# A transformer-block kernel on one core: the first version's row of attention maxima issued by ScalarE, the projection weights on the same queue

## The chip, the cores and the metric

One core of one Trainium2 chip runs the whole program. The metric is device time in microseconds of that core. The kernel before takes 3811.2 us, the median of three runs (3807.66, 3811.2, 3812.2).

## The reference

The input is `x`, four images of 32 x 32 positions with 192 channels, so 4096 tokens. The block computes, one after the other:

```python
x = x + L0_conv(ln(x))      # attention over 1024 positions, 12 heads of 16, with
                            # relative position terms for row and column in the scores
t = t + L0_ffn(ln(t))       # 8 experts, the best 2 of them weighted
x = x + L1_conv(ln(x))      # as L0_conv
t = t + L1_ffn(ln(t))       # attention without position terms, MLP, 4 experts
```

The attention is

```python
attn = einsum('bnqd,bnkd->bnqk', q, k) * scale + bias     # bias: rel_h + rel_w, or none
attn = softmax(attn, axis=-1)
out  = einsum('bnqk,bnkd->bnqd', attn, v)
```

with 48 heads (4 images by 12) of 1024 queries by 1024 keys in each of the three attentions.

## The kernel before

The program is a row of stages with a barrier between them. Three of these are `attention` (line 509): `c0att` and `c1att` with position terms (`rel`), and `f1att` without. A stage works through 24 pairs of heads, and buffers turn in a ring of three (`RING`), so that pair p uses slot p % 3.

**Two streams run side by side in a stage.** The first finds, for every query, a maximum of approximate scores: TensorE multiplies queries by keys (`use_bank`, line 672) into one of three PSUM banks, and VectorE takes the maximum of each 128 x 512 tile (`dve_max`, line 734), 32 tiles for a pair. After the last tile VectorE joins the maxima (lines 739 and 743), TensorE turns them into rows (line 665), and ScalarE copies these out of PSUM into `mrow` (`act_row`, line 747). A DMA then puts the rows, as one row of `qa` on partition 96, beside the queries. With that row in the product the scores come out with the maximum already taken off. The second stream uses them, one pair later: TensorE computes scores of two heads (`score`, line 687), ScalarE their exponential (line 973), and TensorE multiplies by the values (`weigh`, line 700). A pair takes eight steps, `kt` = 0 to 7, one for 128 keys each.

**Versions.** With position terms the keys are split in four quarters, and `qa` holds four versions of the queries, each with its own position rows. Each version needs its own copy of the row of maxima. `place_rows` (line 617) issues them on SyncE's queue, version by version, two heads each: eight DMAs for a pair in `c0att` and `c1att`, two in `f1att`. Version 0 counts on the semaphore `s_at[0]`, the others on `s_at[1]`.

**What waits for what.** `score` at kt 0 waits for `s_at[0]` (line 679), and at kt 2, where version 1 begins, for `s_at[1]` (line 684). Ahead of kt 0, TensorE waits for `s_ld`, the landing of the pair's queries and keys (line 722). The scores of kt 0 belong to the pair before in TensorE's order: they are issued in its step 8. A score product of head h at kt waits for the exponential of the same head at kt - 1 (line 681), since it overwrites it in PSUM. A pair of maxima products waits until VectorE has released the banks (line 660). TensorE's order in one step is: scores of both heads, two maxima products, the weighing product, two maxima products.

**ScalarE's order** (`act_pair`, line 986): the two exponentials of each kt; after kt 0 the copy of the sums of the pair before, after kt 1 a DMA that stores them (line 983); after kt 5 (`ROWS`) the row of maxima of the next pair. At the stage's head it waits for the projection weights (`s_pw`), splits them (line 999), and copies the row of pair 0.

**SyncE's queue** (line 845): at the head the projection weights and the bias (three DMAs), then for each of the three slots the maxima's inputs (`load_maxima`) and the pair's inputs (`load`, 17 DMAs with position terms, nine without), then `refill` for each pair: `place_rows` of pair p - 1, which waits for ScalarE's copy, `load_maxima` of pair p + 1 (ten DMAs), `load` of pair p. GpSimd has a queue of its own, on which every three pairs the sums and their inverses come back.

At the head of a stage VectorE sets ones and zeros (lines 932 to 936), splits the weights (line 941), and then takes all 32 tiles of pair 0 and 14 of pair 1 before the first score product is in TensorE's order (`START`, line 635).

Of the kernel before, what the change touches and what calls it, by code (L numbers as in the profile page):

```python
# [22 lines left out]
B, SIDE, C, NH, HD = 4, 32, 192, 12, 16  # L23
L = SIDE * SIDE
T = B * L
P = 128
# [6 lines left out]
KT = L // P  # L33
QSIDE = SIDE // 2
# [3 lines left out]
HALF, HALVES = C // 2, 2 * B  # L38
# [5 lines left out]
R_REL = 0  # L44
R_QK = 64
R_MAX = 96
R_LOW = 97
# [461 lines left out]
def attention(nc, name, vt, rel, scratch, hot, ident16, by_pool, res, wo, bo, stats=None, room=None, spots=None, spare=None,  # L509
# [6 lines left out]
    with Pool(nc, name) as m:  # L516
        versions = QUARTERS if rel else 1
        qa = room or [m.sb(f"qa{u}", 2 * L, F16) for u in range(RING)]
# [10 lines left out]
        mrow = [m.sb(f"mrow{u}", P, F16, parts=2 * KT) for u in range(RING)]  # L529
# [4 lines left out]
        pw = m.sb("pw", 2 * C, parts=HALF)  # L534
        pwh, pwl = (m.sb(n, 2 * C, F16, parts=HALF) for n in ("pwh", "pwl"))
        bias = m.sb("bias", C)
# [6 lines left out]
        s_pw, s_pwh, s_pwl, s_bias = m.sem("pw"), m.sem("pwh"), m.sem("pwl"), m.sem("bias")  # L543
# [7 lines left out]
        s_ld = [m.sem(f"ld{u}") for u in range(RING)]  # L551
# [3 lines left out]
        s_m16, s_row, s_qm = m.sem("m16"), m.sem("maxrow"), m.sem("qamax")  # L555
        s_s, s_e, s_pv = m.sem("scores"), m.sem("exp"), m.sem("pv")
        s_o, s_at = m.sem("out"), [m.sem(f"maxplaced{k}") for k in range(2)]
# [7 lines left out]
        def queries(h, version, first, count):  # L565
            at = (h * versions + version) * L + first
            return slice(at, at + count)

        def load(sp, pair, u):
            heads = bass.ds(pair * 2, 2)  # L570
            for part, row in ((0, R_QK), (1, R_QK + HD), (0, R_LOW)):
                sp.dma_start(ka[u][row:row + HD, :].rearrange("p (h n) -> p h n", h=2),
                             scratch["qk"][1, heads, part, :, :].rearrange("h r n -> r h n")).then_inc(s_ld[u], 16)
            if not rel:
                for part, row in ((0, R_QK), (0, R_QK + HD), (1, R_LOW)):
                    sp.dma_start(qa[u][row:row + HD, :].rearrange("p (h n) -> p h n", h=2),
                                 scratch["qk"][0, heads, part, :, :].rearrange("h r n -> r h n")
                                 ).then_inc(s_ld[u], 16)
                return
            for h in range(2):  # L580
                head = bass.ds(pair * 2 + h, 1)
                to = qa[u][:, h * versions * L:(h + 1) * versions * L]
                for part, row in ((0, R_QK), (0, R_QK + HD), (1, R_LOW)):
                    src = scratch["qk"][0, head, part, :, :].rearrange("a r n -> (a r) n").unsqueeze(1)
                    sp.dma_start(to[row:row + HD, :].rearrange("p (v n) -> p v n", v=versions),
                                 src.broadcast_to([HD, versions, L])).then_inc(s_ld[u], 16)

                for k in range(2):
                    for half in range(2):
                        row = R_REL + 2 * QSIDE * k  # L590
                        src = scratch["rel"][head, k, half].rearrange("a p r n -> (a p r) n").unsqueeze(1)
                        dst = to[row:row + 2 * QSIDE, :].rearrange("p (u s n) -> p u s n", u=2, s=2)
                        dst = dst[:, half, :, :] if k == 0 else dst[:, :, half, :]
                        sp.dma_start(dst, src.broadcast_to([2 * QSIDE, 2, L])).then_inc(s_ld[u], 16)

        def load_maxima(sp, pair, u):

# [19 lines left out]
        def place_rows(sp, pair, u):  # L617

            sp.wait_ge(s_qm, pair + 1)
            for v in range(versions):  # L620
                for h in range(2):
                    sp.dma_start(qa[u][R_MAX:R_MAX + 1, queries(h, v, 0, L)],
                                 mrow[u][h * KT:(h + 1) * KT, :]).then_inc(s_at[v > 0], 16)

        EARLY = 14
        ROWS = 5
# [102 lines left out]
        def bank_of(u, item):  # L729
            return mps[(len(START) + len(USES) * u + USES.index(item)) % 3]  # L730
# [14 lines left out]
        def act_row(act, pair, u, bank):  # L745
            act.wait_ge(s_row, pair + 1)
            act.activation(mrow[u][:, :], bank[0:2 * KT, 0:P], ACT.Copy).then_inc(s_qm, 1)

        def dve_pair(dve, pair, u, skip=()):
            for item in USES:  # L750
                if item[0] not in skip and item[1] != "row":
                    dve_max(dve, pair + item[0], item[1], bank_of(u, item))
# [91 lines left out]
        with nc.Block() as block:  # L844
            @block.sync
            def _(sp):
                for j in range(2):
                    sp.dma_start(pw[:, j * C:(j + 1) * C], wo[j * HALF:(j + 1) * HALF, :]).then_inc(s_pw, 16)
                sp.dma_start(bias[:, :], bo.broadcast_to([P, C])).then_inc(s_pw, 16)
                for u in range(RING):  # L850
                    for h in range(2 if rel else 0):
                        sp.dma_start(km[u][64 * h + HD:64 * h + 64, :], spots).then_inc(s_lm[u], 16)
# [115 lines left out]
            def _(act):  # L968
# [17 lines left out]
                def act_pair(turn, pair, u, first=False, last=False):  # L986

                    for kt in range(KT):
# [6 lines left out]
                        if kt == ROWS and not last:  # L995
                            act_row(act, pair + 1, (u + 1) % RING, bank_of(u, (1, "row")))

                act.wait_ge(s_pw, 3 * 16)
                act.activation(pwh[:, :], pw[:, :], ACT.Identity, scale=W_SCALE).then_inc(s_pwh, 1)
                act_row(act, 0, 0, mps[START.index((0, "row")) % 3])  # L1000
# [712 lines left out]
```

## Time and profile before

| | |
|---|---|
| median of three runs | 3811.2 us (3807.66 to 3812.2) |
| the profiled execution, its own time | 3804.64 us |
| its span | 3803.1 us |
| TensorE matmul busy | 3146.3 us (83%) |
| VectorE busy | 2664.5 us (70%) |
| ScalarE busy | 2032.5 us (53%) |
| maxima of one attention stage on VectorE (line 734) | 768 tiles of 685 ns |
| exponentials of one attention stage on ScalarE (line 973) | 384 of 1021 ns |

The span goes from the first instruction to the last. An engine's share of it is a mean over stages of different kinds. The three attention stages take the greater part of the time, and the change touches only them.

### The profile page before, as it was taken

What the parts mean: (1) busy time and instruction counts of PE and PEld (TensorE: products, weight loads), DVE (VectorE), ACT (ScalarE), POOL (GpSimd) and SP (SyncE); (2) the same over time, 40 slices, a digit from 0 to 9 for tenths busy, and PEclk for the clock granted to TensorE, in tenths of its full rate; (3) what the DMA queues carried; (4) which work ended last, traced back from release to release, by engine and by line L of the source; (5) the groups of instructions that cost most, each with busy time, mean ns of one, the idle gap of its engine ahead of it and who ended that gap; (6) DMA issues with size and microseconds to landing.
All of it is one profiled execution on the core that took longest, in us unless ns stands there. A gap on an engine that the chain in (4) does not pass through costs nothing. (4 is left out here: it accounts for less than half of the span.)

```text
span 3803.1 us, 66407 instructions
## 1 busy us (share of the span) xinstructions
PE 3146.3 (83%) x20240; PEld 1407.1 (37%) x20240; DVE 2664.5 (70%) x5142; ACT 2032.5 (53%) x2719; POOL 278.2 (7%) x363
## 2 busy tenths in 40 slices
PE   4748999986999999464899998346999996869998
PEld 2422222233666666341222223221222224636666
DVE  5458899966666666445889896638999974556555
ACT  3516677764433333341667676343777773455554
POOL 0010111110000000001011111001111110000000
PEclk9759999997999999675999999576999998979999
DMA  2274667742000000037476764010111111020000
GB/s 59 99 173 83 139 133 144 142 92 72 21 0 0 0 0 0 25 102 173 82 139 131 140 141 98 8 67 27 48 51 44 53 40 28 1 63 9 4 8 13
DMA packets 179968, 251.98 MB, mean 66 GB/s; under 512 B 50974, under 2 KB 73646, under 8 KB 179850
## 3 DMA queue, kind: packets, MB, share of 16 engines
q1 hardware_dynamic: 155642, 213.65, 25.4%
q0 software_dynamic: 13104, 17.60, 2.3%
q10 hardware_dynamic: 11104, 19.28, 1.4%
q8 instruction: 59, 0.97, 0.1%
q14 instruction: 59, 0.48, 0.0%
HBM read 182.80 MB, written 66.65 MB: 66 GB/s over the span
## 5 line engine op out<-in xcount | busy, mean ns | idle before, releaser
L734 DVE TENSOR_REDUCE c1att_mx<-c1att_m 128x1 f32<-128x512 f32 x768 | 493.9, 685 | 64.9 <-PE c1att_m L672 59.7
L734 DVE TENSOR_REDUCE c0att_mx<-c0att_m 128x1 f32<-128x512 f32 x768 | 493.4, 685 | 61.9 <-PE c0att_m L672 56.8
L734 DVE TENSOR_REDUCE f1att_mx<-f1att_m 128x1 f32<-128x512 f32 x768 | 493.3, 685 | 26.5 <-PE f1att_m L672 21.8
L973 ACT ACTIVATE c1att_p<-c1att_s 128x1024 f32<-128x1024 f32 x384 | 372.1, 1021 | 155.7 <-PE c1att_s L687 155.6
L973 ACT ACTIVATE c0att_p<-c0att_s 128x1024 f32<-128x1024 f32 x384 | 372.1, 1021 | 151.9 <-PE c0att_s L687 151.7
L973 ACT ACTIVATE f1att_p<-f1att_s 128x1024 f32<-128x1024 f32 x384 | 372.1, 1021 | 119.6 <-PE f1att_s L687 118.6
L1392 ACT ACTIVATE f_s<-f_u 128x512 f32<-128x512 f32 x192 | 114.6, 597 | 373.5 <-PE f_u L1317 373.5
L1481 DVE SCALAR_TENSOR_TENSOR f_h<-f_u,f_s 128x512 f32<-128x512 f32 x192 | 132.6, 691 | 149.5 <-ACT f_s L1392 145.6
L1400 ACT ACTIVATE moe_h<-moe_u,moe_bu 128x512 f32<-128x512 f32 x192 | 136.5, 711 | 175.8 <-PE moe_u L1317 93.8
L700 PE MATMUL c1att_o<-c1att_p,c1att_vs 128*32 128x512 f32 x1536 | 208.5, 615 | 0.6 <-ACT c1att_p L973 0.6
L700 PE MATMUL c0att_o<-c0att_p,c0att_vs 128*32 128x512 f32 x1536 | 207.5, 613 | 0.6 <-ACT c0att_p L973 0.6
L700 PE MATMUL f1att_o<-f1att_p,f1att_vs 128*32 128x512 f32 x1536 | 206.3, 609 | 0.6 <-ACT f1att_p L973 0.6
L1330 PE MATMUL f_y<-f_dh,xt 128*128 128x192 f16 x1536 | 202.2, 247 | 2.2 <-DVE xt L1437 2.2
L687 PE MATMUL f1att_s<-f1att_qa,f1att_ka 113*128 113x512 f16 x768 | 203.1, 386 | 0.6 <-ACT f1att_p L973 0.3
L1330 PE MATMUL moe_y<-moe_dh,xt 128*128 128x192 f16 x1536 | 195.1, 246 | 0.0
L672 PE MATMUL f1att_m<-f1att_km,f1att_qm 16*128 16x512 f16 x768 | 154.8, 399 | 48.4 <-DVE f1att_ka L936 29.4
L672 PE MATMUL c0att_m<-c0att_km,c0att_qm 64*128 64x512 f16 x768 | 156.2, 403 | 43.4 <-DMA c0att_qm<-rel_parts 24.2
L672 PE MATMUL c1att_m<-c1att_km,c1att_qm 64*128 64x512 f16 x768 | 156.2, 403 | 43.1 <-DMA c1att_qm<-rel_parts 23.9
L1437 DVE TENSOR_TENSOR xt<-moe_h,xt 128x512 f16<-128x512 f32 x192 | 131.3, 691 | 86.3 <-ACT xt L1402 85.3
L1330 PE MATMUL f_y<-f_dl,xt 128*128 128x192 f16 x768 | 189.8, 247 | 0.0
L1330 PE MATMUL moe_y<-moe_dl,xt 128*128 128x192 f16 x768 | 188.9, 246 | 0.0
L687 PE MATMUL c0att_s<-xt,c0att_ka 113*128 113x512 f16 x512 | 135.9, 388 | 31.0 <-DMA xt<-c0att_mrow 28.7
(488 smaller groups left out, 5963.4 us busy)
## 6 DMA issues: line engine op xcount, KB each, us to landing
xt<-rel_parts SPq DMA_DIRECT2D x256, 128.0 KB, 7.4
xt<-qk_parts SPq DMA_DIRECT2D x192, 128.0 KB, 5.0
y<-rel_parts SPq DMA_DIRECT2D x128, 128.0 KB, 5.4
y<-qk_parts SPq DMA_DIRECT2D x96, 128.0 KB, 4.8
c0att_qm<-rel_parts SPq DMA_DIRECT2D x144, 64.0 KB, 2.2
c1att_qm<-rel_parts SPq DMA_DIRECT2D x144, 64.0 KB, 2.2
rel_parts<-c0qkv_rhi SPq DMA_DIRECT2D x48, 128.0 KB, 2.3
rel_parts<-c0qkv_rlo SPq DMA_DIRECT2D x48, 128.0 KB, 2.3
```

The source lines that it names most:

```text
L672: ins = pe.matmul(bank[:, :], qm[v][rows, q0:q0 + P], km[v][rows, c * CHUNK:(c + 1) * CHUNK], start=True, stop=True)
L687: ins = pe.matmul(sps[h][:, c * CHUNK:(c + 1) * CHUNK], ka[u][0:R_END, kcol], qa[u][0:R_END, queries(h, version, c * CHUNK, CHUNK)], start ...
L700: ins = pe.matmul(ops[row:row + 32, :], vs[u][:, (h * KT + kt) * 32:(h * KT + kt + 1) * 32], pr[h][kt % 2][:, c * CHUNK:(c + 1) * CHUNK], ...
L734: dve.tensor_reduce(mx[:, n:n + 1], bank[:, :], AX.X, ALU.max).then_inc(s_mx, 1)
L973: act.activation(pr[h][kt % 2][:, :], sps[h][:, :], ACT.Exp).then_inc(s_e, 1)
L1330: ins = pe.matmul(yps[q % 2][t // 2][:, (t % 2) * C:(t % 2 + 1) * C], hidden[q % 2][:, x], down[:, w], start=k == 0 and i == 0, stop=k == ...
L1392: act.activation(s_buf[i % 2][:, :], ups[i % ring][0][:, :], ACT.Silu, scale=1.0 / W_SCALE).then_inc(s_s, 1)
L1400: act.activation(h32[:, i % 2 * CHUNK:(i % 2 + 1) * CHUNK], bank[:, :], ACT.Gelu, bias=bias, scale=1.0 / W_SCALE).then_inc(s_h32, 1)
L1437: dve.tensor_tensor(hl[q % 2][:, cols], h32[:, i * CHUNK:(i + 1) * CHUNK], hh[q % 2][:, cols], ALU.subtract).then_inc(s_hl, 1)
L1481: dve.scalar_tensor_tensor(out=h32[:, i % 2 * CHUNK:(i % 2 + 1) * CHUNK], in0=ups[i % ring][1][:, :], scalar=1.0 / W_SCALE, in1=s_buf[i % ...
```

## The change

The two DMAs of version 0 move from SyncE's queue to ScalarE's, straight behind the copy that makes the row; SyncE keeps the other versions (six DMAs with position terms, none without). In between ScalarE waits for its own copy. The three DMAs of the projection weights and bias move from SyncE's queue to ScalarE's at the head of a stage. In `load` the same DMAs are issued in another order: by kind and then head, where it was head and then kind.

```diff
-            for h in range(2):
-                head = bass.ds(pair * 2 + h, 1)
-                to = qa[u][:, h * versions * L:(h + 1) * versions * L]
-                for part, row in ((0, R_QK), (0, R_QK + HD), (1, R_LOW)):
...
+            to = qa[u].rearrange("p (h v n) -> p h v n", h=2, v=versions)
+            for part, row in ((0, R_QK), (0, R_QK + HD), (1, R_LOW)):
+                for h in range(2):
...
         def place_rows(sp, pair, u):
 
             sp.wait_ge(s_qm, pair + 1)
-            for v in range(versions):
+            for v in range(1, versions):
                 for h in range(2):
-                    sp.dma_start(qa[u][R_MAX:R_MAX + 1, queries(h, v, 0, L)],
-                                 mrow[u][h * KT:(h + 1) * KT, :]).then_inc(s_at[v > 0], 16)
+                    place_row(sp, u, h, v)
+
+        def place_row(queue, u, h, v):
+            queue.dma_start(qa[u][R_MAX:R_MAX + 1, queries(h, v, 0, L)],
+                            mrow[u][h * KT:(h + 1) * KT, :]).then_inc(s_at[v > 0], 16)
...
             act.activation(mrow[u][:, :], bank[0:2 * KT, 0:P], ACT.Copy).then_inc(s_qm, 1)
+            act.wait_ge(s_qm, pair + 1)
+            for h in range(2):
+                place_row(act, u, h, 0)
...
             def _(sp):
-                for j in range(2):
-                    sp.dma_start(pw[:, j * C:(j + 1) * C], wo[j * HALF:(j + 1) * HALF, :]).then_inc(s_pw, 16)
-                sp.dma_start(bias[:, :], bo.broadcast_to([P, C])).then_inc(s_pw, 16)
...
+                for j in range(2):
+                    act.dma_start(pw[:, j * C:(j + 1) * C], wo[j * HALF:(j + 1) * HALF, :]).then_inc(s_pw, 16)
+                act.dma_start(bias[:, :], bo.broadcast_to([P, C])).then_inc(s_pw, 16)
                 act.wait_ge(s_pw, 3 * 16)
```

## Rows read from the trace of the kernel before

**Rows 1.** Groups by line: VectorE's maxima in steady stretches, `f1att` then `c0att` (busy, idle before).

```profile
L734 DVE TENSOR_REDUCE f1att_mx<-f1att_m 128x1 f32<-128x512 f32 x702 | 450.8, 684 | 16.8 <-PE f1att_m L672 12.2
...
L734 DVE TENSOR_REDUCE c0att_mx<-c0att_m 128x1 f32<-128x512 f32 x703 | 451.6, 685 | 37.8 <-PE c0att_m L672 32.9
```

**Rows 2.** ScalarE's copy of the rows by line: count, ns, first and last start.

```profile
L747 ACT ACTIVATE f1att_mrow<-f1att_m x23: 266/266/267, 2634.5 to 3117.8; 16x128 f16<-16x128 f32 x23
...
L747 ACT ACTIVATE c0att_mrow<-c0att_m x22: 266/266/267, 332.9 to 811.9; 16x128 f16<-16x128 f32 x22
```

**Rows 3.** TensorE's waits, steady stretches of `c0att` and `c1att` (total us, times, longest).

```profile
PE c0att_s L687 <- DMA xt<-c0att_mrow: 13.5, 6, 2.7
...
PE c0att_s L687 <- DMA xt<-rel_parts: 1.9, 1, 1.9
PE c0att_s L687 <- DMA y<-c0att_mrow: 1.9, 2, 1.1
...
PE c1att_s L687 <- DMA xt<-c1att_mrow: 10.5, 6, 2.3
PE c1att_s L687 <- DMA y<-c1att_mrow: 4.3, 2, 2.3
PE c1att_s L687 <- DMA y<-rel_parts: 2.0, 1, 2.0
```

**Rows 4.** The wait of SyncE's queue in steady `c0att` (total us, times, longest).

```profile
SPq L622 <- ACT c0att_mrow L747: 117.4, 23, 18.6
```

**Rows 5.** Timeline of one pair of `c0att` (start us, us, instructions, idle before).

```profile
514.09 0.27 ACT L747 ACTIVATE c0att_mrow<-c0att_m 16x128 f16<-16x128 f32 x1 [0.77 <-PE c0att_m L665]
...
514.38 5.42 SPq L622 DMA_DIRECT2D xt<-c0att_mrow  x8
...
514.70 1.94 ACT L973 ACTIVATE c0att_p<-c0att_s 128x1024 f32<-128x1024 f32 x2 [0.35 <-PE c0att_s L687]
...
515.47 5.21 DVE L734 TENSOR_REDUCE c0att_mx<-c0att_m 128x1 f32<-128x512 f32 x8 [0.48 <-PE c0att_m L672]
...
516.69 1.04 PE L687 MATMUL c0att_s<-xt,c0att_ka 113*128 113x512 f16 x4
...
517.66 0.39 PE L672 MATMUL c0att_m<-c0att_km,c0att_qm 64*128 64x512 f16 x2
...
522.03 1.89 PE L687 MATMUL c0att_s<-xt,c0att_ka 113*128 113x512 f16 x4 [2.67 <-DMA xt<-c0att_mrow]
```

**Rows 6.** That pair's load: issues, time to landing, and a window (DMA share last but one).

```profile
L594 SPq DMA_DIRECT2D xt<-rel_parts x8: 317/376/384, 506.4 to 511.2; - x8
...
DMA to landing us min/median/max: 3.5/8.7/10.3
...
520.50:521.00 0.50, 0.00 (x0) 0.00 (x0) 0.19 (x1) 0.00 (x0) 0.00 (x0) 1.00 0.16 13
```

**Rows 7.** The head of `c0att`: timeline, then windows (granted clock, DMA share, GB/s last).

```profile
242.98 1.83 DVE L941 SCALAR_TENSOR_TENSOR c0att_pwl<-c0att_pw,c0att_pwh 96x384 f16<-96x384 f32 x1
...
293.15 1.87 PE L687 MATMUL c0att_s<-xt,c0att_ka 113*128 113x512 f16 x4 [15.24 <-DMA xt<-c0att_mrow]
...
295.28 1.95 PE L687 MATMUL c0att_s<-xt,c0att_ka 113*128 113x512 f16 x4 [0.26 <-ACT c0att_p L973]
...
300.00 1.04 PE L687 MATMUL c0att_s<-xt,c0att_ka 113*128 113x512 f16 x4
...
295.00:296.00 1.00, 0.74 (x3) 0.13 (x2) 0.00 (x0) 1.00 (x2) 0.00 (x0) 0.50 0.01 2
...
298.00:300.00 2.00, 2.00 (x11) 0.12 (x3) 1.10 (x2) 0.29 (x1) 0.00 (x0) 0.54 0.00 0
```

**Rows 8.** ScalarE's own DMA issues by line (ns: shortest, median, longest): `f1att`, `c1att`, gates.

```profile
L983 ACTq DMA_DIRECT2D o_sums<-f1att_o x22: 338/343/357, 2643.4 to 3104.7; - x22
...
L983 ACTq DMA_DIRECT2D o_sums<-c1att_o x22: 338/365/384, 1841.7 to 2323.0; - x22
...
L1064 ACTq DMA_DIRECT2D moe_gw<-in_f_gate x2: 360/438/517, 3349.1 to 3349.5; - x2
```

More of the change, by code:

```diff
@@ L579, in load @@
                 return
-            for h in range(2):
-                head = bass.ds(pair * 2 + h, 1)
-                to = qa[u][:, h * versions * L:(h + 1) * versions * L]
-                for part, row in ((0, R_QK), (0, R_QK + HD), (1, R_LOW)):
[L584 to L594, printed above, removed]
+            to = qa[u].rearrange("p (h v n) -> p h v n", h=2, v=versions)
+            for part, row in ((0, R_QK), (0, R_QK + HD), (1, R_LOW)):
+                for h in range(2):
+                    src = scratch["qk"][0, bass.ds(pair * 2 + h, 1), part, :, :].rearrange("a r n -> (a r) n")
+                    sp.dma_start(to[row:row + HD, h], src.unsqueeze(1).broadcast_to([HD, versions, L])
+                                 ).then_inc(s_ld[u], 16)
+            for k in range(2):
+                for half in range(2):
+                    row = R_REL + 2 * QSIDE * k
+                    dst = to[row:row + 2 * QSIDE].rearrange("p h (u s) n -> p h u s n", u=2)
+                    for h in range(2):
+                        src = scratch["rel"][bass.ds(pair * 2 + h, 1), k, half].rearrange("a p r n -> (a p r) n")
+                        sp.dma_start(dst[:, h, half] if k == 0 else dst[:, h, :, half],
+                                     src.unsqueeze(1).broadcast_to([2 * QSIDE, 2, L])).then_inc(s_ld[u], 16)
         def load_maxima(sp, pair, u):
@@ L747, in act_row @@
             act.activation(mrow[u][:, :], bank[0:2 * KT, 0:P], ACT.Copy).then_inc(s_qm, 1)
+            act.wait_ge(s_qm, pair + 1)
+            for h in range(2):
+                place_row(act, u, h, 0)
         def dve_pair(dve, pair, u, skip=()):
```

## The prediction

> **What bounds the kernel now.** I read the groups by line first, then waits, then single pairs in the timeline. In the steady part of an attention stage VectorE is the bound: in a stretch of 484 us of `f1att` its maxima are busy 450.8 us, with 16.8 us of idle ahead of them [rows 1]. The small reductions, reciprocals and their gaps are the rest. In `c0att` the same number of tiles has 37.8 us of idle. The starts of the row copies give the length of a pair: (3117.8 - 2634.5) / 22 = 21.97 us in `f1att` and (811.9 - 332.9) / 21 = 22.81 us in `c0att` [rows 2]. So the position stages lose 0.84 us a pair, or some 18 us in 22 pairs. The waits say where: TensorE stalls nine times in the steady part of `c0att`, 13.5 + 1.9 + 1.9 = 17.3 us, and nine times in `c1att`, 10.5 + 4.3 + 2.0 = 16.8 us [rows 3]. Together that is 34.1 us. `f1att` has no such stall.
>
> The row is named as releaser, but it is not what is late. In the pair shown, the load's last DMA is issued at 511.2 and the longest landing took 10.3 us, which gives 521.5 at most, and by 520.5 the DMA share has fallen to 0.16 [rows 6]. TensorE goes on at 522.03 [rows 5]. The row, issued at 514.38, lands just behind its queue's load, some 0.3 us later; one stall of each stage has the load itself as releaser [rows 3].
>
> At a stage's head the row costs more. TensorE sits idle 15.24 us before 293.15, though its maxima are done and pair 0's inputs were loaded long ago: the row stands behind the loads of slots 1 and 2 [rows 7].
>
> **The change, part by part.**
>
> *Row of pair 0, early.* On its own queue the row can land before TensorE asks at about 277.9 (293.15 - 15.24), so kt 0 and 1 run in the idle time. Then kt 2 waits for version 1, whose rows still stand behind the loads on SyncE. The DMA share is 0.01 from 295, so they land between 293 and 295; I take 294. Before, kt 2 began at 300.0 [rows 7]. The gain is less than 6 us, since the granted clock is at its lower level (0.5, 1.2 GHz) until just before 300 [rows 7], after which it is whole. TensorE had been busy for 6.5 us then, and I let it pay the same again. At the lower level a step takes 300.00 - 295.28 = 4.7 us against 2.6 (four tiles of 5.21 us for eight [rows 5]), so in 6 us it does 1.3 steps, worth 3.4 us. In two stages: **-6.8 us**. `f1att` has no such wait: nothing. The bounds are 0 (the row lands no earlier) and 2 x 6 = 12.
>
> *Two DMAs fewer on SyncE.* A row DMA takes 5.42 / 8 = 0.68 us [rows 5]. `load_maxima` and `load` of the next pair are issued 1.36 us earlier, as SyncE waits for nothing but ScalarE's copy (5.1 us a pair, 117.4 in 23) [rows 4], and that wait keeps the place. Since the engines are full, the load lands earlier by the same. With the 0.3 us of the row, and scores that want the load later by what ScalarE loses (next part), a stall shortens by up to 2.3 us; 18 stalls have a mean of 1.9 and a longest of 2.7 [rows 3]. Where stall follows stall, the next is wanted earlier when the first goes; for these and the longest I leave 5 us. **-29 us**. Bounds: -34 (all gone), and -11 if the load lands no earlier and only the row's part and ScalarE's delay shorten them (0.3 x 18, and some 0.3 more each). VectorE would wait next, as in `f1att`.
>
> *Two DMAs more on ScalarE, and a wait.* This is the price, and it stands on the path in all three stages. Behind the copy stand the exponentials of kt 6. Before: copy ends 514.36, exponential at 514.70 [rows 5]. After: wait and two issues of 0.68, so 514.36 + 0.05 + 1.36 = 515.8. The two exponentials end at 517.7 (1.94 for both). The scores of kt 7 overwrite what they read: head 0 could go at 516.9 for 516.69 before, head 1 at 517.8 for 517.13 (half-way through its 1.04). Two more products of 0.22, and the maxima products start at 518.25 instead of 517.66 [rows 5]: 0.6 us late. Their place is tight: before, they ended at 517.66 + 0.39 = 518.05, and VectorE took them as its fifth tile at 515.47 + 4 x 0.65 = 518.08. A bound engine does not make it up: **0.6 us a pair**. ScalarE catches up in its idle time of the next steps, so it is once a pair. `f1att`: 23 x 0.6 = 13.8 us. In the position stages SyncE issues its six rows in the same moment; ScalarE's store takes 365 ns beside SyncE's issues in `c1att` and 343 in `f1att`, the gate's 438 [rows 8]. I take 0.04 each, nearest to the store in the same loop, so 0.67: 46 x 0.67 = 30.8. **+44.6 us**. Bounds a pair: 0 if an issue cost 0.34 as the store does (exponential at 515.1, just within what the scores allow), and 1.1, the whole delay of the exponential.
>
> The Trainium skill (Perfetto Trace Analysis, DMA Instruction, HWDGE) says that the descriptor generator is locked for exclusive use while one sequencer uses it. By that rule each of ScalarE's issues may have to wait for one of SyncE's; the store's 365 against 343 ns agrees in direction, not in size, and the sum would be the fourth case below.
>
> *Weights on ScalarE's queue.* ScalarE is idle there, and VectorE splits the weights at 242.98 without idle before it, behind its own zeros [rows 7]. The three issues cost nothing; if the weights came after that, each microsecond would count in three stages. SyncE starts its loads some 1.3 us earlier, which only helps version 1's rows. *Order in `load`:* the same 14 DMAs, one semaphore; nothing, within 0.5 us a load either way.
>
> **Sum.** -6.8 - 29 + 44.6 = +8.8 us. Against the profiled execution: 3804.6 + 8.8 = 3813.4. That execution stands 6.6 us below the median, so for the median 3811.2 + 8.8 = **3820.0 us**, slower by 0.23%. A measurement of this kernel tells about 0.2%, 7.6 us, from no change.
>
> **Rivals.**
>
> 1. *The delay of ScalarE is hidden* (faster). Its issue costs 0.34, or the scores have more room. Then nothing is paid, stalls shorten by 1.7 instead of 2.3 us (some 10 us stay): -6.8 - 24 = -31, **3780**. Below 0.52 us a pair ((6.8 + 29) / 69) the change gains. For it: ScalarE has idle time before most exponentials. Against it: the same DMA takes 0.68 us on SyncE whatever the load. Partly hidden, 0.4 a pair, gives -6.8 - 27 + 27.6 = -6, 3805. 17%.
>
> 2. *Gains and price even out* (no change): the 0.6 holds with nothing on top, and nearly all stalls go. 69 x 0.6 - 6.8 - 33 = +1.6, **3813**. 33%, with the near half of my own case.
>
> 3. *The load lands no earlier.* The DMA engines are full from before its last issue, and GpSimd's transfers take the room freed. Then 18 us of stalls more stay: **3838**. Against it: the engines come to a rest between loads. 10%.
>
> 4. *The two queues hold each other up.* Each of ScalarE's issues costs 0.2 to 0.3 us more while SyncE issues: 46 x 0.5 = 23, less 3 by shorter stalls: **3840**. The gate's 438 ns speaks for a part, the store against. 12%.
>
> The rest, 28%, is the forecast itself, ending between 3816 and 3830.
>
> **Numbers.** Faster by over 0.2%: 0.18. Within 0.2%: 0.34. Slower: 0.48. Range 3798 to 3836: it takes in the evening-out, most of a part-hidden price and most of rival 3.
>
> **What would show it.** Between ScalarE's row copy and the next exponential: 1.4 us, with two DMA issues of some 0.68 us (0.34 would be rival 1; 0.9 or more rival 4). VectorE's idle ahead of a tile some 4 us behind the row: 0.6 us in each pair, `f1att` included, its pair 22.6 us instead of 21.97. TensorE's waits for the row gone, those for the load left with under 8 us in two stages; over 20 would be rival 3. At the head of `c0att` the first score at 278, kt 2 at about 294. If the pair of `f1att` keeps 21.97 us, my main step is wrong.

## The result and the profile after

| | before | after |
|---|---|---|
| median | 3810.74 us (3803.83 to 3815.27, 6 runs) | 3831.04 us (3823.89 to 3838.45, 6 runs) |
| ratio, 95% interval | | 1.0053 [1.0037, 1.0069] |
| the profiled execution | 3804.64 us | 3838.45 us |
| `f1att`: end of row copy 0 to first score of pair 23 | 515.3 us | 530.3 us |
| `c0att`, the same | 547.0 us | 562.5 us |
| `c1att`, the same | 550.6 us | 552.4 us |

The change makes the kernel slower by 0.53%, some 20 us. The last three rows run from the end of ScalarE's first row copy to the start of TensorE's first score product of the last pair. They hold 23 pairs each and grow by 15.0 + 15.5 + 1.8 = 32.3 us, where the two profiled executions differ by 33.8. So all but 1.5 us of the difference lies in the attention stages. The profiled execution after is the slowest of its six, 7.4 us above their median, and that of before lies 6.1 us below its own. A single execution therefore shows the terms some 13 us too large in all. It also scatters by stage: where an experiment below leaves a stage's rows and loads as they were, its profile has 509.4 to 515.3 us for `f1att`, and in experiments 3 and 9 the position stages take 552 to 558 us, where the kernel before has 547.0 and 550.6.

**VectorE waits longer in each pair.** First the groups by line of the kernel after, VectorE's maxima in a steady stretch of `f1att` (columns as in [rows 1]).

```profile
L737 DVE TENSOR_REDUCE f1att_mx<-f1att_m 128x1 f32<-128x512 f32 x701 | 450.5, 685 | 31.9 <-PE f1att_m L675 27.7
```

The busy time is that of [rows 1], and the idle ahead of it has grown from 16.8 to 31.9 us. That is 15.1 us in 22 pairs, 0.69 each; over the whole stage it is 42.0 for 26.5, where experiments 2, 3 and 10, which leave this stage alone, have 23.9 to 26.6. Nothing in the steady part of `f1att` has changed but the issuer of two DMAs and ScalarE's wait ahead of them. Between row copies the undisturbed pair has gone from 21.67 to 22.44 us (medians; [rows 2] give the mean with the disturbed pairs in it).

The timeline of one such pair of the kernel after shows the place (start, us, instruction, idle before).

```profile
2969.23 0.27 ACT L750 ACTIVATE f1att_mrow<-f1att_m 16x128 f16<-16x128 f32 x1 [0.77 <-PE f1att_m L668]
2969.53 1.32 ACTq L625 DMA_DIRECT2D f1att_qa<-f1att_mrow  x2
...
2971.03 3.77 ACT L976 ACTIVATE f1att_p<-f1att_s 128x1024 f32<-128x1024 f32 x4 [1.54 <-PE f1att_s L690]
...
2972.11 0.61 PE L690 MATMUL f1att_s<-f1att_qa,f1att_ka 113*128 113x512 f16 x2 [0.21 <-ACT f1att_p L976]
...
2973.03 0.60 PE L690 MATMUL f1att_s<-f1att_qa,f1att_ka 113*128 113x512 f16 x2 [0.31 <-ACT f1att_p L976]
...
2973.99 1.29 DVE L737 TENSOR_REDUCE f1att_mx<-f1att_m 128x1 f32<-128x512 f32 x2 [0.77 <-PE f1att_m L675]
```

Read it downwards. The copy ends at 2969.50. The two issues hold ScalarE's sequencer until 2970.85, and the exponential starts 0.18 us after that. It has been idle for 1.54 us where [rows 5] show 0.35, although its scores were ready. The exponentials of kt 6 come late, the score products of kt 7 wait for them (0.21 and 0.31), the maxima products behind these are late too, and VectorE stands idle for 0.77 us. The profile names `f1att_s` as releaser of the exponential. What held it was the row of ACTq just above.

The position stages show the same with a slightly longer hold. Timeline of one pair of `c0att` after:

```profile
523.32 0.27 ACT L750 ACTIVATE c0att_mrow<-c0att_m 16x128 f16<-16x128 f32 x1 [0.77 <-PE c0att_m L668]
523.62 4.06 SPq L625 DMA_DIRECT2D xt<-c0att_mrow  x6
523.62 1.51 ACTq L625 DMA_DIRECT2D xt<-c0att_mrow  x2
...
525.32 2.86 ACT L976 ACTIVATE c0att_p<-c0att_s 128x1024 f32<-128x1024 f32 x3 [1.73 <-issue]
```

The two issues take 1.51 us beside SyncE's six, and the idle is 1.73. The middle pair is 22.53 us in `c0att` and 22.51 in `c1att`, where the undisturbed pair before has 21.69 in both. Pairs without a stall run from 22.3 to 22.8 us here, so the 0.84 and 0.82 are good to some 0.1.

By line, the row DMAs of the kernel after (ns: shortest, median, longest) say that this prolongation is small in most pairs.

```profile
L625 ACTq DMA_DIRECT2D f1att_qa<-f1att_mrow x48: 627/632/703, 2624.8 to 3150.9; - x48
L625 ACTq DMA_DIRECT2D xt<-c0att_mrow x32: 627/648/1236, 269.4 to 804.0; - x32
```

**The stalls have become shorter, but not gone.** TensorE's waits of the kernel after, in steady `c0att` and in steady `c1att` (total us, times, longest):

```profile
PE c0att_s L690 <- ACT c0att_p L976: 13.3, 42, 0.8
PE c0att_s L690 <- DMA xt<-c0att_mrow: 11.5, 6, 4.7
...
PE c1att_s L690 <- ACT c1att_p L976: 14.0, 44, 1.1
...
PE c1att_s L690 <- DMA xt<-c1att_mrow: 5.8, 6, 1.5
```

Over a whole stage the stalls for load and rows, with those that the view calls `issue` (1.5 us before in `c1att`, 0.7 after in each stage), go from 17.3 to 12.2 us and from 18.2 to 6.6. In place of what went stands the wait for ScalarE (13.3 and 14.0), two for each pair. The row is still the last to arrive. In the pair of `c0att` shown above the load's last issue is at 518.42 and its longest landing took 11.7 us, so 530.1; TensorE goes on at 531.33, 1.2 us later, where in the pair of [rows 5] and [rows 6] it was 0.5. By the semaphore events of the trace the row lands behind its load in all 14 stalled pairs, in `c0att` by 0.35 to 1.37 us (before, on the load's own queue, by 0.16 to 0.40).

```profile
L593 SPq DMA_DIRECT2D xt<-rel_parts x8: 317/376/388, 515.1 to 518.4; - x8
...
DMA to landing us min/median/max: 6.8/10.4/11.7
...
531.33 1.10 PE L690 MATMUL c0att_s<-xt,c0att_ka 113*128 113x512 f16 x4 [1.77 <-DMA xt<-c0att_mrow]
```

**The head gives less than hoped.** Head of `c0att` after, timeline and two windows (granted clock third from the end):

```profile
269.37 1.94 ACTq L625 DMA_DIRECT2D xt<-c0att_mrow  x2
...
280.57 1.87 PE L690 MATMUL c0att_s<-xt,c0att_ka 113*128 113x512 f16 x4 [2.22 <-DMA xt<-c0att_mrow]
...
297.97 1.46 PE L690 MATMUL c0att_s<-xt,c0att_ka 113*128 113x512 f16 x3 [10.85 <-DMA xt<-c0att_mrow]
...
298.00:300.00 2.00, 2.00 (x6) 0.50 (x6) 0.00 (x0) 0.96 (x2) 0.00 (x0) 0.50 0.02 4
300.00:303.00 3.00, 3.00 (x13) 0.44 (x12) 1.45 (x3) 0.98 (x2) 0.00 (x0) 0.50 0.00 0
```

The first score now starts at 280.57 instead of 293.15 [rows 7]. But kt 2 waits for version 1 until 297.97, for 300.00 before, and the clock is at its lower level (0.50, 1.2 GHz) there. It is whole only from 303.5, 5.5 us behind the start of kt 2; before, it was whole from 299.8, just ahead of kt 2 [rows 7]. From the end of the first row copy to kt 2 it is 28.6 us instead of 31.1, and in `c1att` 30.0 instead of 31.5.

### The profile page after: what moved, and what is told of

Its sections match the earlier page's. It is cut to its first block and busy times, and to the rows that moved or that the text cites. A ratio compares the mean times of both kernels' runs of the same rounds, so it can differ in the third digit from the quotient of the medians.

```text
span 3836.9 us, 66408 instructions
## 1 busy us (share of the span) xinstructions
PE 3163.0 (82%) x20240; PEld 1406.1 (37%) x20240; DVE 2663.8 (69%) x5142; ACT 2025.3 (53%) x2719; POOL 279.2 (7%) x363
## 5 line engine op out<-in xcount | busy, mean ns | idle before, releaser
L690 PE MATMUL c0att_s<-xt,c0att_ka 113*128 113x512 f16 x512 | 140.6, 393 | 35.5 <-DMA xt<-c0att_mrow 24.6
```

What stands on the lines that cost most here:

```text
L690: ins = pe.matmul(sps[h][:, c * CHUNK:(c + 1) * CHUNK], ka[u][0:R_END, kcol], qa[u][0:R_END, queries(h, version, c * CHUNK, CHUNK)], start ...
```

## The experiments

Two causes were before me after this profile. The theory: ScalarE's hold is paid in every pair; the row's own queue and SyncE's shorter list give some of it back; and the new order of the load, which the forecast had at nothing, costs about half of what is measured. The rival causes were that the order is innocent, or that the price is a matter of two queues rather than of ScalarE's place in the chain. "Lag" below is the time from a load's last issue to its landing, as a median over the pairs of slot 0 and over those of slot 1. Slot 2 is left out of these figures: in the old order its lags fall in two groups, some 5 to 7 and 9 to 13 us, whose shares change from kernel to kernel, so that its median jumps between them. The ratio is always to the kernel before, run on the same chip.

**1. The change with the old order of the load** (`e1_old_order`).

```diff
-            for part, row in ((0, R_QK), (0, R_QK + HD), (1, R_LOW)):
-                for h in range(2):
...
+            for h in range(2):
+                for part, row in ((0, R_QK), (0, R_QK + HD), (1, R_LOW)):
...
```

> The changed kernel with the order of the DMAs in load put back to head and then kind. Theory A (the new order makes the loads slow): the time from the last issue of a load to its landing in c0att, 6.9 to 7.1 us in quiet pairs and 11.1 to 12.1 us in crowded ones after the change, falls back to the 5.9 and 9.4 to 10.6 us of before; the stalls for the load, some 12 us in c0att, nearly vanish; at the head of c0att kt 2 starts at 295 instead of 298; pairs without a stall keep 22.5 us. Together 10 to 20 us faster than the changed kernel, 3811 to 3821. Theory B (the order is innocent, the loads are slow since they start earlier and meet the stores and GpSimd's transfers): landings and time stay as after the change, 3831.

Measured: 3820.52 us (3817.66 to 3826.03), ratio 1.0019 [1.0008, 1.0031]. Against the change that is 10.5 us by the medians, which come from two chips, and 13 by the ratios, whose intervals do not meet. The change and this run differ by the order alone. Stalls over a stage: 5.7 us in `c0att` and 0.9 in `c1att`. Lag 5.6 and 9.1 us, where the kernel after has 7.0 and 11.4; the single values do not overlap (5.2 to 6.3 against 6.8 to 7.6, 8.6 to 9.7 against 11.1 to 12.1). Slot 2 goes the other way, 10.3 against 7.5, so that the mean over all pairs differs by no more than 0.5 us, and by 0.1 in `c1att`. TensorE's waits in steady `c0att`:

```profile
PE c0att_s L690 <- ACT c0att_p L976: 13.5, 43, 0.8
...
PE c0att_s L690 <- DMA y<-c0att_mrow: 3.7, 2, 2.4
PE c0att_s L690 <- DMA xt<-c0att_mrow: 1.9, 1, 1.9
```

The wait for ScalarE is that of the kernel after, and the DMAs' is half of theirs there (5.6 us for 11.5). The undisturbed pair stays at about 22.5 us in the position stages and 22.44 in `f1att`, so the price of ScalarE has nothing to do with the order.

**2. The new order alone, in the kernel before** (`e2_order_only`).

```diff
-            for h in range(2):
-                for part, row in ((0, R_QK), (0, R_QK + HD), (1, R_LOW)):
...
+            for part, row in ((0, R_QK), (0, R_QK + HD), (1, R_LOW)):
+                for h in range(2):
...
```

> The kernel before with nothing but the new order of the DMAs in load. Theory A: a load lands 1.0 to 1.5 us later after its last issue, in c0att and c1att alone; 18 stalls grow by that, so 15 to 25 us slower than before, 3826 to 3836; f1att keeps its pair of 21.67 us. Theory B: no difference, 3811.

Measured: 3823.38 us (3811.21 to 3836.62), ratio 1.0037 [1.0022, 1.0052], 14 us. `f1att` keeps its 21.67 us a pair; the waits in steady `c0att` grow from the 17.3 us of [rows 3] to 23.4:

```profile
PE c0att_s L687 <- DMA xt<-c0att_mrow: 15.8, 6, 5.2
PE c0att_s L687 <- DMA xt<-rel_parts: 4.2, 2, 2.4
PE c0att_s L687 <- DMA y<-c0att_mrow: 3.4, 3, 1.8
```

Lag 6.7 and 10.5 us, for 6.1 and 9.9 before (6.0 to 6.2 and 9.9 to 10.0 in experiments 3 and 9, which keep order and list). So the order costs alone about what it does within the change, though the lag grows by less.

**3. The weights alone on ScalarE's queue** (`e3_weights_only`).

```diff
             def _(sp):
-                for j in range(2):
-                    sp.dma_start(pw[:, j * C:(j + 1) * C], wo[j * HALF:(j + 1) * HALF, :]).then_inc(s_pw, 16)
-                sp.dma_start(bias[:, :], bo.broadcast_to([P, C])).then_inc(s_pw, 16)
...
+                for j in range(2):
+                    act.dma_start(pw[:, j * C:(j + 1) * C], wo[j * HALF:(j + 1) * HALF, :]).then_inc(s_pw, 16)
+                act.dma_start(bias[:, :], bo.broadcast_to([P, C])).then_inc(s_pw, 16)
```

> The kernel before with nothing but the projection weights and bias issued by ScalarE. Theory A (off the path: VectorE sets its zeros until 242.98 and only then wants the split weights; the loads start 1.3 us earlier): 0 to 3 us faster, 3809 to 3812; the first maximum of c0att starts as before, 9.7 us after VectorE's first memset. Rival (the weights come later beside the loads and VectorE waits for them): up to 2 us slower in each of three stages, 3818.

Measured: 3806.02 us (3797.6 to 3813.74), ratio 0.9988 [0.9975, 1.0001]. No difference that the measurement can tell, at most a small gain. The first maximum of `c0att` starts 9.5 us behind VectorE's first memset, for 9.6 before.

**4. ScalarE's two issues, but one behind each exponential of kt 6** (`e4_hidden_issue`), against the kernel of experiment 1.

```diff
             act.activation(mrow[u][:, :], bank[0:2 * KT, 0:P], ACT.Copy).then_inc(s_qm, 1)
-            act.wait_ge(s_qm, pair + 1)
-            for h in range(2):
-                place_row(act, u, h, 0)
...
+                            if kt == ROWS + 1 and not last:
+                                if h == 0:
+                                    act.wait_ge(s_qm, pair + 2)
+                                place_row(act, (u + 1) % RING, h, 0)
```

> The changed kernel with the old order in load, and ScalarE's two row DMAs put one behind each exponential of kt 6 instead of ahead of both. Theory A (the price is that ScalarE's sequencer holds the exponentials back while it issues; an issue of 0.63 us fits under an exponential of 1.02 us): the pair of f1att returns from 22.44 to 21.7 us, quiet pairs of c0att from 22.5 to 21.7; the row lands some 4.5 us after its copy, just in time for scores at 4.9. With the load 1.36 us earlier the stalls fall to half: 3785 to 3797. Rival (the price is the transfer or the semaphore traffic on ScalarE's side, or any DMA issued there): the pair of f1att stays at 22.4 us, time as in the run with the old order.

Measured: 3780.01 us (3773.56 to 3788.58), ratio 0.9911 [0.9896, 0.9927]. The same DMAs on the same queue, each behind an exponential instead of both ahead of them, are worth 40 us. Timeline of a pair of `f1att`:

```profile
2904.97 0.27 ACT L750 ACTIVATE f1att_mrow<-f1att_m 16x128 f16<-16x128 f32 x1 [1.57 <-PE f1att_m L668]
2905.58 1.02 ACT L973 ACTIVATE f1att_p<-f1att_s 128x1024 f32<-128x1024 f32 x1 [0.35 <-PE f1att_s L690]
2905.61 1.47 ACTq L625 DMA_DIRECT2D f1att_qa<-f1att_mrow  x2
...
2906.50 1.02 ACT L973 ACTIVATE f1att_p<-f1att_s 128x1024 f32<-128x1024 f32 x1
```

The issues start while the exponential runs: the sequencer is held, the activation behind it is not. The idle is 0.35 us again, and the pair 21.67 us. This decides for the place in the chain and against the queues as such. The stalls, though, are back: 11.8 and 16.0 us in the position stages, for 5.7 and 0.9 in experiment 1. Most of what experiment 1 had gained there was not an earlier load, then, but longer pairs. The pairs of slot 1, where most stalls are, show it. These are medians of seven pairs of `c0att`, from issues and semaphore events, in us from the end of ScalarE's row copy:

| | load's last issue | load landed | row landed | first score |
|---|---|---|---|---|
| before | -3.2 | 6.7 | 6.8 | 7.1 |
| experiment 2 | -3.2 | 7.3 | 7.1 | 7.4 |
| experiment 4 | -4.5 | 5.2 | 5.7 | 5.9 |
| experiment 1 | -5.2 | 3.7 | 4.2 | 5.8 |
| the change | -5.2 | 6.2 | 6.9 | 7.1 |
| experiment 6 (below) | -6.1 | 3.2 | 3.4 | 4.9 |

Without a stall the scores start at 4.9 us, in experiment 1 and the change at some 5.7 to 5.8. Two issues fewer bring the load's issue forward by 1.3 us and its landing by 1.5 (experiment 4). With pairs that are 0.8 us longer both come earlier again against the copy, and the demand comes later (experiment 1). The new order takes 2.5 us of the landing away again (the change).

**5. Only the row of pair 0 on ScalarE's queue** (`e5_first_row_only`), in the kernel before.

```diff
-                place_rows(sp, 0, 0)
+                place_rows(sp, 0, 0, 1)
...
+                act.wait_ge(s_qm, 1)
+                for h in range(2):
+                    act.dma_start(qa[0][R_MAX:R_MAX + 1, queries(h, 0, 0, L)],
+                                  mrow[0][h * KT:(h + 1) * KT, :]).then_inc(s_at[0], 16)
```

> The kernel before, with version 0's row of pair 0 alone issued by ScalarE at the head of each stage; every other row on SyncE as before. Theory A: no price in the steady part (pair of f1att 21.67 us), kt 2 of pair 0 in c0att and c1att starts at 295 instead of 300 and the lower clock takes part of it back: 3.4 us each, 7 us in all, 3804. Rival: the idle 10 us before kt 2 cost as much as the early steps bring, 3811.

Measured: 3804.53 us (3796.91 to 3810.79), ratio 0.9978 [0.9967, 0.9989], a gain of 8.4 us. Head of `c0att`:

```profile
278.27 1.87 PE L687 MATMUL c0att_s<-xt,c0att_ka 113*128 113x512 f16 x4 [0.86 <-DMA xt<-c0att_mrow]
...
295.26 1.46 PE L687 MATMUL c0att_s<-xt,c0att_ka 113*128 113x512 f16 x3 [11.27 <-DMA xt<-c0att_mrow]
```

These are the 278 and, within 1.3 us, the 294 of the forecast. Alone, the step does what it was said to do. In the change both are later (280.57, 297.97). With the old order (experiment 1) kt 2 comes 28.4 and 27.1 us after the first row copy, for 28.6 and 30.0 with the new one. That tells little: experiment 4 has the same program as experiment 1 up to there, and its kt 2 comes 24.6 and 28.2 us after the copy.

**6. One DMA for both heads' rows, all on SyncE** (`e6_merged_sync`), in the kernel before. In `qa` the queries lie by version, then head, so that the rows of both heads are one run, and a pair has four row DMAs instead of eight.

```diff
-            at = (h * versions + version) * L + first
+            at = (version * 2 + h) * L + first
...
-                for h in range(2):
-                    sp.dma_start(qa[u][R_MAX:R_MAX + 1, queries(h, v, 0, L)],
-                                 mrow[u][h * KT:(h + 1) * KT, :]).then_inc(s_at[v > 0], 16)
+                place_row(sp, u, v)
+
+        def place_row(queue, u, v):
+            queue.dma_start(qa[u][R_MAX:R_MAX + 1, 2 * v * L:2 * (v + 1) * L],
+                            mrow[u][:, :]).then_inc(s_at[v > 0], 16)
```

> The kernel before, all rows on SyncE, but qa laid out version by version so that one DMA places both heads' rows: four issues instead of eight, ScalarE untouched. Theory A (rows in the steady part are late because SyncE issues the next load late; which queue carries version 0 matters little): a load is issued 2.7 us earlier than before, the stalls of 35 us in two stages fall below 10, the pair of f1att stays 21.67: 3780 to 3788. Rival (version 0 needs a queue of its own): its row still lands behind the load, stalls shrink only by a fourth, 3800.

Measured: 3759.07 us (3752.64 to 3761.05), ratio 0.9856 [0.9836, 0.9876], 55 us faster. A stall of 0.5 us in `c1att` is all that is left. Position stages 523.2 and 528.8 us for 547.0 and 550.6. Version 0 needs no queue of its own: without touching ScalarE, four issues fewer do far more than the two fewer of the change. In slot 1 of `c0att` the load's last issue comes 2.9 us earlier and the load lands 3.5 us earlier (the table above), ahead of the demand at 4.9. Most of that is SyncE's shorter list; the rest, a lag that is shorter by some 0.5 us, may come of the other layout or of fewer row DMAs, which no run separates. The gain is over 20 us larger than expected: VectorE's idle ahead of its maxima falls by 45 us in the two stages (61.9 and 64.9 to 37.9 and 44.1) where TensorE's stalls fall by 35. An issue with both rows takes 0.51 us in `f1att` and 0.59 in the position stages (medians).

**7. The same merging in the kernel of experiment 1** (`e7_merged_ahead`): one issue stands ahead of the exponentials on ScalarE. The edit of experiment 6, and

```diff
             act.wait_ge(s_qm, pair + 1)
-            for h in range(2):
-                place_row(act, u, h, 0)
+            place_row(act, u, 0)
```

> The changed kernel with the old order in load and one DMA for both heads, so ScalarE holds one issue instead of two ahead of the exponentials of kt 6. Theory A (the price is the length of ScalarE's hold, less the 0.43 us that the scores of kt 7 leave): the exponential starts 0.86 us after the copy instead of 1.5 to 1.7, the pair of f1att falls from 22.44 to 21.75, 0.1 above the kernel before; with the stalls mostly gone 3778 to 3790. Rival (a fixed price for any DMA issued there): 22.1 or more in f1att, 3800.

Measured: **3743.88 us** (3741.57 to 3754.37), ratio **0.9824** [0.9805, 0.9842], the fastest of all. The undisturbed pair is 21.68 us in `f1att` and 21.69 and 21.70 in the others. Timeline of a pair of `f1att`:

```profile
3061.57 0.27 ACT L749 ACTIVATE f1att_mrow<-f1att_m 16x128 f16<-16x128 f32 x1 [1.68 <-PE f1att_m L667]
...
3061.86 0.53 ACTq L624 DMA_DIRECT2D f1att_qa<-f1att_mrow  x1
...
3062.49 1.94 ACT L974 ACTIVATE f1att_p<-f1att_s 128x1024 f32<-128x1024 f32 x2 [0.66 <-PE f1att_s L689]
```

The exponential is idle for 0.66 us instead of 0.35, so it is 0.31 us late, and this costs nothing. In the kernel after it is 1.54 - 0.35 = 1.19 us late and costs 0.77. If lateness beyond the room is paid in full, the chain has some 1.19 - 0.77 = 0.42 us of room, and 0.31 lies within it. VectorE's idle ahead of the maxima, over the whole of each stage, stands in the profile's costliest groups:

```profile
L736 DVE TENSOR_REDUCE c1att_mx<-c1att_m 128x1 f32<-128x512 f32 x768 | 493.7, 686 | 35.9 <-PE c1att_m L674 30.9
L736 DVE TENSOR_REDUCE c0att_mx<-c0att_m 128x1 f32<-128x512 f32 x768 | 493.7, 686 | 35.7 <-PE c0att_m L674 30.6
L736 DVE TENSOR_REDUCE f1att_mx<-f1att_m 128x1 f32<-128x512 f32 x768 | 493.6, 685 | 22.7 <-PE f1att_m L674 18.1
```

In the kernel before they are 64.9, 61.9 and 26.5. The 15 us over experiment 6 are mostly the heads: kt 2 comes 25.5 and 25.2 us after the row copy, for 29.2 and 33.9 (24.2 and 26.8 in experiment 8). The time lies 34 us below the 3778 to 3790 expected: as in experiment 6, the merging was worth more than I had counted.

**8. Merging, with the issue behind the exponential** (`e8_merged_hidden`), experiment 4's place with experiment 6's edit.

```diff
+                            if kt == ROWS + 1 and h == 0 and not last:
+                                act.wait_ge(s_qm, pair + 2)
+                                place_row(act, (u + 1) % RING, 0)
```

> Merged rows as in the two runs above, version 0 on ScalarE behind the first exponential of kt 6, the other three on SyncE. Theory A: no price (f1att 21.67 us), a load issued 3.4 us earlier than before, stalls nearly gone, head of c0att and c1att 3 to 6 us shorter: 3768 to 3778. Rival (the load's landing is limited by the DMA engines, not by its issue): as the run with the hidden issues, 3780.

Measured: 3749.29 us (3745.55 to 3751.96), ratio 0.983 [0.9813, 0.9846]. Not to be told from experiment 7: where one issue fits in the room, hiding it brings nothing.

**9. The price by itself: rows on ScalarE ahead of the exponentials in `f1att` alone** (`e9_price_f1att`), all else as before.

```diff
-            for v in range(versions):
+            for v in range(0 if rel else 1, versions):
...
+            if not rel:
+                act.wait_ge(s_qm, pair + 1)
+                for h in range(2):
+                    place_row(act, u, h, 0)
```

> The kernel before, with the rows of f1att alone issued by ScalarE ahead of the exponentials, as in the change; weights, order and the position stages as before. Theory A (the price alone): the pair of f1att 22.44 instead of 21.67 us, VectorE idle 0.77 us ahead of one tile in each pair, 23 x 0.77 = 18 us slower, 3829. Rival (part of the loss in f1att came from the other edits): under 10 us slower, 3820.

Measured: 3829.02 us (3824.67 to 3831.9), ratio 1.0056 [1.0041, 1.0072], 21 us. The pair of `f1att` is 22.44 us, and the stage 527.8 for 515.3. The profile's group of `f1att`'s maxima has 40.3 us of idle, for 26.5 before:

```profile
L737 DVE TENSOR_REDUCE f1att_mx<-f1att_m 128x1 f32<-128x512 f32 x768 | 493.6, 685 | 40.3 <-PE f1att_m L675 35.8
```

The price stands in a stage without position rows, where SyncE has no row to place. 23 x (22.44 - 21.67) = 18 us, inside the interval (16 to 27 us). The stage by the profile gives 12.5 against the kernel before, whose 515.3 is the longest of the unchanged ones, and 13 to 18 against the others (509.4 to 514.8).

**10. Another order of the load, in the kernel before** (`e10_alternating`): within a head a DMA of queries and one of position rows by turns, so that no DMA follows one to the same partitions.

```diff
+                shared(0, R_QK)
+                placed(0, 0)
+                shared(0, R_QK + HD)
+                placed(1, 0)
+                shared(1, R_LOW)
+                placed(0, 1)
+                placed(1, 1)
```

> The kernel before with a third order in load: head and then kind, but shared and position rows in turn, so that no DMA follows one that writes the same partitions. Theory C (DMAs to the same partitions back to back are what makes the new order slow): a load lands sooner than before after its last issue, below 5.9 us in quiet and below 9.5 us in crowded pairs; stalls fall, 3795 to 3806. Rival (it is not the partitions but the heads: reading one head's data in one go is what is fast): landings and time as before, 3812.

Measured: 3790.97 us (3785.95 to 3793.99), ratio 0.9958 [0.9942, 0.9973], 16 us faster. Lag 5.6 and 9.1 us. Within the 14 DMAs of a load, no DMA here follows one to the same partitions; in the order of before four do, in that of the change nine. The lags of slot 0 in the kernels with SyncE's full list are 5.6, 6.1 and 6.7 us, and the ratios 0.9958, 1 and 1.0037. The stalls of both stages come to 31 us, for 35.5 before and 41 and 43 in experiments 3 and 9. Slot 2 stands apart here too (9.5 us for 6.2 before). The landing times of the position rows agree. For experiment 10, the kernel before, and experiment 2, in this order (us: shortest, median, longest):

```profile
DMA to landing us min/median/max: 3.1/6.7/10.9
```

```profile
DMA to landing us min/median/max: 3.3/6.9/11.0
```

```profile
DMA to landing us min/median/max: 6.1/8.9/11.9
```

The order of the change also puts all position rows last, which raises their own landing by itself. The lag of the whole load is the fair measure.

**11. That order in the kernel of experiment 7** (`e11_merged_alternating`).

> The fastest run so far (merged rows, version 0 by ScalarE ahead of the exponentials, 3744) with that third order. Theory C: the stalls are gone there already, so only the head gains, where kt 2 of pair 0 waits for the loads of slots 1 and 2: 0 to 4 us faster, 3740 to 3744. Rival: no difference.

Measured: 3748.7 us (3745.17 to 3751.87), ratio 0.9847 [0.983, 0.9864], against a kernel before that ran at 3806.22. The lag falls from 5.5 and 8.6 to 5.1 and 8.0 us, and the time does not fall: there was no stall left to shorten.

## Why the prediction was right, and where its terms were not

The time, 3831.0 us, lies in the range and on the side that had most of the chance, 11.0 us above the forecast of 3820.0. Experiment 1, the change without the term that I had set at nothing, came to 3820.5. That it meets the forecast to half a microsecond is in part luck: its interval is 9 us wide, and the terms fit less well than that number. Here they are by the stages of one execution each: the stalls, then the time from row copy to kt 2 at the heads, and what is left of the stages' growth.

| | forecast | experiment 1 | the change |
|---|---|---|---|
| ScalarE's hold (the rest) | +44.6 | +49.4 | +52.9 |
| stalls of the position stages | -29 | -28.9 | -16.7 |
| heads | -6.8 | -7.1 | -3.9 |
| sum by stages | +8.8 | +13.4 | +32.3 |
| by the ratio | | +7 (3 to 12) | +20 (14 to 26) |

The kernel before is the weak side of this table. Its profile has 35.5 us of stalls, where experiments 3 and 9 have 41 and 43 in the same position stages; against the mean of the three, experiment 1 saves 33 us of stalls and the change 21, and the first line hardly moves (49 and 53). The heads scatter by up to 4 us between executions of the same program. So -28.9 for -29 says that the size is right, not that it is right to a tenth.

**Two DMAs more on ScalarE.** Right in mechanism and place, stage by stage and with the idle at VectorE, and too small: 0.77 us a pair where I had 0.6, and 0.84 and 0.82 where I had 0.67. I was right about the issue (0.63 us for the 0.68 of SyncE's row) and the room (0.42 us, 0.5 taken). Half of what I missed is the time behind the last issue: the exponential starts 0.18 us after it, where I had allowed 0.05 for the wait and nothing there, so that it is 1.19 us late instead of 1.1. The other half is the smaller room. By the pairs the term is 23 x (0.77 + 0.84 + 0.82) = 56 us. Rival 1 fell with experiment 9, but its number, 3780, is what experiment 4 gave once the issue really stood under an exponential. That the two numbers agree is chance in part: of the 24 us of stalls that rival 1 counted on, the profile of experiment 4 shows 8 gone. In that sense the forecast's "below 0.52 us a pair the change gains" was the useful sentence.

**The load order.** This is the step that failed. "Nothing, within 0.5 us a load either way" had its argument in the count of DMAs and the one semaphore. The lag in `c0att` grew by 1.4 us in slot 0 and 2.3 in slot 1 from experiment 1 to the kernel after, and by 0.6 in both slots from the kernel before to experiment 2. The term that I had at nothing thus measures 10.5 to 13 us within the change and 14 alone, half or more of the 20 us. The stage terms show where it went: 12 us of stalls that had gone in experiment 1 stand again. The 3 us at the heads are within the scatter there.

**Two DMAs fewer on SyncE.** The size came out as forecast, without the order (-28.9 for -29), but its reason only in part. Experiment 4 has the two DMAs fewer and no delay on ScalarE, and its profiled execution still has 27.8 us of stalls, of 35.5. So some 8 us come from the earlier load, net, and 21 from the longer pairs, which I had listed as the smaller part. The earlier load itself went as I had it (issued 1.3 us earlier, landed 1.5 us earlier, in slot 1 of `c0att`). The 0.3 us of the row did not: on its own queue the row lands a median of 0.8 us behind its load in the stalled pairs of experiment 4, for 0.34 in `c0att` before, so that part of the gain is lost on the row. Rival 3 is not right either: experiments 4 and 6 show that a load issued earlier lands earlier.

**Row of pair 0, early.** The mechanism was right by itself (experiment 5: 278 and 295 us at the head, and a gain of 8.4 us for 6.8). With the old order it came out at 7.1 us by the heads, in the change at 3.9. Whether the load order makes this difference, since the rows of version 1 stand behind the loads, is not shown: experiments 1 and 4, with the same program up to kt 2, differ by 3.8 us in `c0att` and 1.1 in `c1att`. The row itself lands at 280.4 in the change and not before 277.9. The clock took back what I had let it take, 5.5 us at the lower level behind kt 2 for 6.5 (4.0 in experiment 5).

**Weights.** Nothing, as forecast (experiment 3).

**The signs.** Two DMA issues and 1.54 us between copy and exponential (1.4 forecast), VectorE idle in each pair, the mean pair of `f1att` at 22.61 us (22.6): these came. The waits for the row are not gone, and with 18.8 us the stalls stand just under the 20 that were to speak for rival 3. The load order is what put them there, not a load that keeps its old time.

**Rival 4** had a time near the result (3840), but not the cause. The median of ScalarE's issues is 0.648 us in `c0att` against 0.632 in `f1att`, 0.02 more and not 0.2 to 0.3 (slot 2 has 0.637, `c1att` 0.652 and 0.654). In a single pair it can be more: 1.51 us for two in the one above, against 1.32. The Trainium skill (Perfetto Trace Analysis, DMA Instruction, HWDGE) has the descriptor generator locked for exclusive use. The longer pair agrees in direction. In the pair of `f1att` shown above, however, SyncE issues a DMA of 0.33 us at 2969.69, wholly within ScalarE's first, and neither is prolonged, so by this trace the lock cannot cover the whole time that the profile gives to an issue.

**What stays open.** Why DMAs to the same partitions, one behind the other, land later: three orders rank as the count of such neighbours would have them, but they differ in other things too, as in which rows come last. Why a row on a queue of its own lands further behind its load than one behind it in the same queue. And what makes the heads scatter between executions of one program.

## What to carry to other kernels

A DMA issue is an instruction of the queue that issues it. Ahead of compute on the critical chain it cost its full hold here (0.63 us each and 0.18 behind) less the room there, and behind an activation, under which it ran, nothing. So measure the room in the chain first (here 0.42 us), and count issues before moving them: one DMA for two rows beat every placement of two. And where loads run close to their deadline, the order of a load's DMAs is a change of its own, to be costed or tried alone.

## What the hardware showed that I had not expected

- **A queue of its own did not bring a small DMA past crowded engines.** At the head of `c0att` ScalarE issues the row from 269.37 to 271.31, and TensorE gets it at 280.57, over 9 us later, with SyncE's loads under way. In the steady part it lands 0.35 to 1.37 us behind the load in the stalled pairs of `c0att`, where the row on the load's own queue came 0.16 to 0.40 behind. In `f1att`, where the engines are free, it lands about 2.5 us after ScalarE's copy. The Trainium skill (DMA: Bandwidth & Descriptors, Issuing engines are not separate DMA queues) says that DMAs of all issuers run on the same 16 engines and interleave, and that a second issuer saves only sequencer time. The trace agrees: what the second issuer brought was a load issued 1.3 us earlier (experiment 4). The same page (Queues, rings and completion order) says that an engine takes turns between its queues packet by packet, by which I would have had the row well ahead of the loads; in the kernel after it is so in none of the 14 stalled pairs.
- **One issue for 16 partitions costs less than one for eight, twice.** Two row DMAs from eight partitions each take 1.27 us to issue (2 x 0.632), one from sixteen 0.54 (510 to 552 ns in `f1att`), while DMAs of the load take 0.32 to 0.38.
- **The order of DMAs within one load** moves its landing in slots 0 and 1 by 0.5 to 2.3 us and the kernel by 0.3 to 0.4%, with the same bytes, count and queue.
